# Second batch's shares of the last MLP pieces behind the other batch's, the very last product in two banks, and the plain output rows two to a step

## The chip, the cores and the metric

The kernel runs on one core of a Trainium2 chip. The metric is the device time of one execution in microseconds (us). The engines are TensorE (PE, with its weight loads as PEld), VectorE (DVE), ScalarE (ACT), GpSimd (POOL) and SyncE (SP), which here only issues DMAs.

## The reference, cut to what matters

Two layers on x of shape (2, 1024, 512): block-banded attention with a layer norm, then a routed layer. The routed layer picks 128 of 1024 rows of each batch, runs attention and a gated MLP on these 256 rows, mixes the result into the rows, and a second layer norm goes over everything. The change is in the MLP and behind it:

```
x1 = x + attn_out                                   # the 2 x 128 selected rows
h2 = _rms_norm(x1, ln2_w)
mlp = jax.nn.silu(h2 @ w_gate) * (h2 @ w_up) @ w_down   # 512 -> 2048 -> 512
processed = x1 + mlp
gated = gate * processed + (1.0 - gate) * x
output = hidden_states.at[b, idx].set(gated)        # the other rows stay as they are
return _layernorm(x + output)                       # over all rows
```

## The kernel before

The kernel writes the program of each engine itself. A planner calls `job(kind, key)` in one global order; each engine then walks through the jobs that have a part for it, in that order. So the order of the calls is the order of the work on every engine. `SIGNALS` lists the steps that a job completes on each engine, waits refer to them by name, and `hold`/`freed` make a job wait until the last user of a buffer or PSUM bank is done with it.

All products are made in three passes (high part by high part, high by low, low by high), so each float32 operand is split in two. A weight piece of 128 x 1024 is loaded by SP into one of three raw buffers (line 1893; the load of piece n waits for the low part of piece n - 3), rounded by ACT (line 1288), and the remainder is taken by POOL (line 1808) or DVE (line 1492), which alternate in the MLP.

The MLP (from `gate_up(c)` at line 753 and `down(c)` at line 764) has 8 steps c of 256 hidden columns. A step has a gate piece, an up piece, a down piece and two activation tiles, `gu` 2c and 2c + 1. For a tile TensorE makes gate and up for both batches (24 matmuls of 256 columns in bank proj0 or proj1). ACT applies silu (line 1470), DVE multiplies (line 1753), ACT rounds (line 1288), POOL takes the remainder (line 1855), all for 256 rows at once. `down(c)` then adds the two tiles of step c times piece `d2` c to the sums of batch 0 (bank s0) and batch 1 (bank s1), six matmuls of 512 columns for each. The planner calls `down(c - 1)` behind the tiles of step c, and `down(7)` last. In the stream of weight pieces, numbered through the whole kernel, step c has g2, u2 and then d2 of c - 1; the last ones are 84 (g2 of 7), 85 (u2 of 7), 86 (d2 of 6) and 87 (d2 of 7). POOL takes the low part of pieces with even numbers here, DVE that of odd ones. The high parts of the pieces that a step has loaded are planned at its end, behind the output row below.

Beside this, rows that were not selected go out: `plnorm` of batch 1 scales a tile of 128 rows on ACT (line 1384) and stores it (SP, line 1917, 256 KB). There are eight of them, `plain[0]` to `plain[7]`. Step c appends `plain[c]` to the running generators; two ticks later it is emitted, so tiles 0 to 4 go out at steps 2 to 6, and the last three behind `down(7)`.

The end: `fin` b on DVE adds the MLP sum of batch b to the residual already mixed (lines 1763, 1765, 1766: sum, statistics, aggregate), POOL makes the inverse root (lines 1781, 1783), `finrow` b on DVE normalises the row (line 1771), and POOL scatters the 128 rows of batch b (line 1868), after all stores of plain rows have landed. The jobs stand in the order fin 0, fin 1, finrow 0, finrow 1.

## Time and profile before

| | us |
|---|---|
| median of 3 runs | 1295.19 |
| lowest and highest | 1294.98, 1295.84 |
| the profiled execution's own time | 1295.61 |
| its span, from first to last instruction | 1293.8 |

In that execution TensorE was busy 98% of the span, VectorE 61%, ScalarE 46%, GpSimd 19%; its mean granted clock was 0.995 of full speed. Of the chain that ended last, 89% is TensorE and 5% DVE. The timeline rows read: start in us from the span's start, duration in us, engine, line of the kernel, operation, what it writes and reads with its shape, how many in a row, and in brackets how long the engine had been idle before and what released it. A row in which the same line occurs several times is merged.

### The profile page before, as it was taken

Reading aid. Unit: us, or ns where it says so; the run is one execution under the profiler, and the core shown is the slowest. Engines: PE = TensorE matmul, PEld = TensorE weight load, DVE = VectorE, ACT = ScalarE, POOL = GpSimd, SP = SyncE. Lnnn points to the kernel's source line nnn. Section 1 sums busy time; section 2 is a strip of 40 time slices with the busy share of each in tenths; the row PEclk is TensorE's granted clock in tenths of the full one; section 3 lists DMA queues with packets and bytes.
Section 4 is the critical chain, followed back from the end, with each engine's and each line's share of the span. In section 5 each row is a group of like instructions: output and inputs, shape, how many; then the busy total and the mean of one; then the engine's idle time right before and its main releaser. Section 6 shows DMA issues by size and latency. Waiting matters only on the chain.

```text
span 1293.8 us, 19096 instructions
## 1 busy us (share of the span) xinstructions
PE 1267.4 (98%) x7356; PEld 1091.0 (84%) x7356; DVE 784.0 (61%) x2189; ACT 600.5 (46%) x1424; POOL 244.2 (19%) x218
## 2 busy tenths in 40 slices
PE   9999999999999999999999999999999999999897
PEld 8898989898989898987789898989898985546696
DVE  5556565656665656667676766565655579744243
ACT  5544445454444444545544444444444443525353
POOL 2101111111111110224220202020201106100154
PEclk9999999999999999999999999999999999999899
DMA  6101101010101012013320100200010135582253
GB/s 203 34 17 33 34 33 33 30 37 20 47 17 50 33 50 65 17 41 115 109 95 17 49 18 13 75 33 34 27 32 26 35 123 177 190 287 96 88 190 138
DMA packets 62443, 89.34 MB, mean 69 GB/s; under 512 B 3264, under 2 KB 36032, under 8 KB 62352
## 3 DMA queue, kind: packets, MB, share of 16 engines
q1 hardware_dynamic: 61936, 86.82, 20.2%
q0 software_dynamic: 416, 1.31, 0.3%
q8 instruction: 57, 0.93, 0.3%
q14 instruction: 34, 0.28, 0.1%
HBM read 79.20 MB, written 8.91 MB: 68 GB/s over the span
## 4 chain that ended last, share of the span: by engine, by line
PE 89%; DVE 5%; ACT 3%; DMA 1%; issue 1%; POOL 0%; SPq 0%; POOLq 0%; ACTq 0%
PE proj L1008 42%; PE y L1008 13%; PE s L1008 10%; PE o L1008 9%; PE tp L1097 6%; PE proj L1016 4%; PE s L1016 2%; DVE arena L1492 2%; ACT arena L1288 1%; PE o L1016 1%; ACT prob L1326 1%; DVE products L1608 1%; DVE prob L1527 1%; DVE yacc L1579 1%; DMA late<-rope,position 1%
## 5 line engine op out<-in xcount | busy, mean ns | idle before, releaser
L1008 PE MATMUL proj<-arena 128*128 128x256 f32 (+1 forms) x3408 | 623.8, 332 | 2.9 <-DVE arena L1492 2.8
L1008 PEld LDWEIGHTS proj<-arena 128*128 128x128 f32 x3408 | 521.0, 190 | 60.0 <-DVE arena L1492 4.5
L1326 ACT ACTIVATE prob<-prob,stat 128x384 f32<-128x384 f32 (+1 forms) x256 | 151.0, 590 | 428.9 <-DVE stat L1527 428.9
L1808 POOL TENSOR_TENSOR arena<-wraw,arena 128x1024 fp32r<-128x1024 f32 x75 | 181.9, 2434 | 826.2 <-ACT arena L1288 826.2
L1492 DVE TENSOR_TENSOR arena<-proj,arena 128x512 fp32r<-128x512 f32 (+1 forms) x256 | 142.5, 557 | 267.6 <-ACT arena L1288 264.9
L1008 PE MATMUL y<-arena 128*128 128x512 f32 x810 | 210.7, 395 | 0.3 <-DVE yacc L1579 0.3
L1492 DVE TENSOR_TENSOR arena<-tp,arena 128x384 fp32r<-128x384 f32 (+2 forms) x258 | 134.7, 522 | 100.8 <-ACT arena L1288 100.5
L1008 PE MATMUL o<-arena 128*128 128x256 f32 (+2 forms) x960 | 194.6, 322 | 0.0
L1008 PE MATMUL s<-arena 128*128 128x384 f32 (+2 forms) x870 | 191.1, 333 | 2.2 <-DVE arena L1492 2.1
L1288 ACT ACTIVATE arena<-proj 128x512 fp32r<-128x512 f32 (+1 forms) x256 | 124.1, 485 | 114.9 <-PE proj L1008 111.9
L1008 PEld LDWEIGHTS y<-arena 128*128 128x128 f32 x810 | 146.6, 188 | 24.8 <-DVE yacc L1579 0.7
L1008 PEld LDWEIGHTS s<-arena 128*128 128x128 f32 x870 | 151.3, 188 | 19.1 <-DVE arena L1492 3.5
L1008 PEld LDWEIGHTS o<-arena 128*128 128x128 f32 x960 | 136.8, 190 | 0.7 <-DVE arena L1492 0.2
L1527 DVE CUSTOM_DVE_ANT_0 prob<-s,band 128x384 f32<-128x384 f32 (+1 forms) x256 | 131.6, 514 | 0.7 <-PE s L1008 0.7
L1288 ACT ACTIVATE arena<-tp 128x384 fp32r<-128x384 f32 (+2 forms) x258 | 118.0, 457 | 12.9 <-PE tp L1097 10.4
L1097 PE MATMUL tp<-ident,prob 128*128 128x128 f32 x704 | 119.3, 273 | 2.3 <-DVE prob L1536 2.3
L1536 DVE TENSOR_SCALAR prob<-prob,stat 128x384 f32<-128x384 f32 (+1 forms) x256 | 111.8, 437 | 9.1
L1097 PEld LDWEIGHTS tp<-ident,prob 128*128 128x128 f32 x704 | 85.9, 140 | 18.6 <-DVE prob L1536 7.8
L1579 DVE TENSOR_TENSOR yacc<-y,yacc 128x512 f32<-128x512 f32 x127 | 87.1, 686 | 13.6 <-PE y L1008 13.4
L1288 ACT ACTIVATE arena<-wraw 128x1024 fp32r<-128x1024 f32 (+1 forms) x90 | 91.0, 1036 | 5.8 <-DMA wraw<-in_L_ffn_w_gate 3.6
L1288 ACT ACTIVATE arena<-o 128x512 fp32r<-128x512 f32 (+1 forms) x74 | 42.1, 569 | 32.7 <-PE o L1179 22.7
L1016 PE MATMUL proj<-late 128*128 128x512 f32 x120 | 56.4, 598 | 0.0
(158 smaller groups left out, 691.1 us busy)
## 6 DMA issues: line engine op xcount, KB each, us to landing
wraw<-in_L_attn_Wv SPq DMA_DIRECT2D x16, 512.0 KB, 3.3
wraw<-in_L_attn_Wo SPq DMA_DIRECT2D x16, 512.0 KB, 3.7
late<-in_L_ffn_wq SPq DMA_DIRECT2D x16, 512.0 KB, 6.4
late<-in_L_ffn_wo SPq DMA_DIRECT2D x16, 512.0 KB, 4.7
wraw<-in_L_attn_Wq SPq DMA_DIRECT2D x15, 512.0 KB, 3.3
wraw<-in_L_attn_Wk SPq DMA_DIRECT2D x15, 512.0 KB, 3.4
yacc<-in_L_attn_hidden_states SPq DMA_DIRECT2D x16, 256.0 KB, 3.1
y_dram<-yacc SPq DMA_DIRECT2D x16, 256.0 KB, 3.1
```

Source lines behind the costliest of these rows:

```text
L1008: ins = e.matmul(out_ap, l[a], r[b], start=first and i == 0 and j == 0, stop=final and i == n - 1 and j == 2, skip_group_check=skip)
L1016: ins = e.matmul(out_ap, l, r, start=first and i == 0, stop=final and i == n - 1, skip_group_check=skip)
L1097: ins = e.transpose(bank["tp"][:, m * P:(m + 1) * P], prob[i % 2][:, m * P:(m + 1) * P], ident[:])
L1288: e.activation(dst, src, ACT.Copy).then_inc(*S_.inc(*name, "hi"))
L1326: e.activation(prob[s][:, 0:n], prob[s][:, 0:n], ACT.Exp, bias=stat[:, 4 * s + 1:4 * s + 2], scale=-1.0, accum_out=stat[:, 4 * s + 2:4 * s ...
L1492: e.tensor_tensor(dst_lo, src, dst_hi.bitcast(F32), ALU.subtract).then_inc(*V_.inc(*name, "lo"))
L1527: e.tensor_tensor_reduce(prob[s][:, 0:n], bank[f"s{s}"][:, 0:n], reach, -SCALE, -NEG, ALU.add, ALU.min, nm).then_inc(*V_.inc("scores", H, ...
L1536: e.tensor_scalar(prob[s][:, 0:n], prob[s][:, 0:n], rc, None, ALU.mult).then_inc(*V_.inc("norm", H, i, "prob"))
L1579: e.tensor_tensor(yacc[:, t, :], bank[bank_of["out", G, t]][:, :], yacc[:, t, :], ALU.add).then_inc(*V_.inc("out", G, t, "sum"))
L1608: e.tensor_tensor_reduce(products[:], row, router[:], 1.0, 0.0, ALU.mult, ALU.add, score[:, c:c + 1]).then_inc(*V_.inc("lnscore", b, t, "s ...
L1808: e.tensor_tensor(lo, wraw[n % RAW_SLOTS][:], hi.bitcast(F32), ALU.subtract).then_inc(*G_.inc("wsplit", n, "lo"))
```

## The change

The share of each batch in a down piece is a job of its own now: `down(b, c)`. For steps 1 to 5 the two shares follow each other as before. In step 6 only batch 0's share of piece 5 is planned, and in step 7 none. Behind the last tile come batch 1's share of piece 5, batch 0's shares of pieces 6 and 7, batch 1's of piece 6, and a new job `downend`: batch 1's product with piece 7, in two halves of 256 columns in two other banks (`y` and `o1`). On DVE, batch 1's sum is taken in three parts: `finsum` adds what bank s1 holds, `finend` adds each half and takes its statistics, and aggregates both. The plain rows are appended two to a step, in steps 0 to 3, so they are emitted two each at steps 2 to 5.

```diff
-        def down(c):
-            need("d2", 0, c)
+        def down(b, c):
+            if b == 0:
+                need("d2", 0, c)
             if c == 0:
-                for b in range(NB):
-                    hold(f"s{b}", ("down", 0), V_, "fin", b, "sum")
-            job("down", c)
-            retire(("d2", 0, c), "down", c, f"made{NB - 1}")
+                hold(f"s{b}", ("down", b, 0), V_, "finsum" if b else "fin", b, "sum")
+            job("down", b, c)
+            if b == NB - 1:
+                retire(("d2", 0, c), "down", b, c, "made")
...
         for c in range(FF // GW):
             gate_up(c)
-            if c >= 1:
-                down(c - 1)
+
+            if 1 <= c < FF // GW - 1:
+                down(0, c - 1)
+            if 1 <= c < FF // GW - 2:
+                down(1, c - 1)
             was_loaded = loaded_to[0]
             tick()
-            running.append([plain[c], None])
+            for t in range(2 * c, min(2 * c + 2, TT)):
+                running.append([plain[t], None])
             split_loaded(was_loaded)
-        down(FF // GW - 1)
+        down(1, FF // GW - 3)
+        for c in (FF // GW - 2, FF // GW - 1):
+            down(0, c)
+        down(1, FF // GW - 2)
+
+
+        for half, to in enumerate(ENDS):
+            hold(to, ("downend", half), V_, "finend", 1, ("left", "right")[half])
+        job("downend")
...
+                elif kind == "downend":
+                    c = FF // GW - 1
+                    w2 = [z.rearrange("p (k n) -> p k n", k=2) for z in weights("d2", 0, c)]
+                    pe.wait_ge(*split("d2", 0, c))
+                    pe.wait_ge(*G_.at("gu", 2 * c + 1, "lo"))
+                    for half, name in ((0, "left"), (1, "right")):
+                        cols = slice(half * GW, (half + 1) * GW)
+                        pe.wait_ge(*freed(ENDS[half], "downend", half))
+                        ins = three_passes(e, bank[ENDS[half]][:, cols],
+                                           [([aT[(2 * c + f) % A_SLOTS][z][:, P:2 * P] for z in range(2)],
+                                             [w2[z][:, f, cols] for z in range(2)]) for f in range(2)], True, True)
+                        ins.then_inc(*T_.inc("downend", name))
...
+                elif kind == "finend":
+                    b, = key
+                    y1 = work[4 + b]
+                    dve.wait_ge(*V_.at("finsum", b, "sum"))
+                    dve.wait_ge(*freed(f"moments{b}", "finend", b))
+                    dve.wait_ge(*freed(f"share{b}", "finend", b))
+                    for half, name in ((0, "left"), (1, "right")):
+                        cols = slice(half * GW, (half + 1) * GW)
+                        dve.wait_ge(*T_.at("downend", name))
+                        after(e.scalar_tensor_tensor(y1[:, cols], bank[ENDS[half]][:, cols], gate[:, 4 * b + 1:4 * b + 2], y1[:, cols],
+                                                     ALU.mult, ALU.add), "finend", b, name)
+                        after(e.bn_stats(halves[:, 6 * half:6 * half + 6], y1[:, cols]), "finend", b, f"{name}stats")
+                    e.bn_aggr(mv[b][:], halves).then_inc(*V_.inc("finend", b, "moments"))
```

TensorE from the tiles of step 6 (12 and 13) to its last instruction, before. proj0 and proj1 are the tiles, s0 and s1 the sums of batch 0 and 1:

```order
L1008 MATMUL proj0<-arena 128x256 x24
L1008 MATMUL proj1<-arena 128x256 x24
L1008 MATMUL s0<-arena 128x512 x6
L1008 MATMUL s1<-arena 128x512 x6
L1008 MATMUL proj0<-arena 128x256 x24
L1008 MATMUL proj1<-arena 128x256 x24
L1008 MATMUL s0<-arena 128x512 x6
L1008 MATMUL s1<-arena 128x512 x6
L1008 MATMUL s0<-arena 128x512 x6
L1008 MATMUL s1<-arena 128x512 x6
```

The same of the changed kernel (its line 1031 is line 1008 of before):

```order
L1031 MATMUL proj0<-arena 128x256 x24
L1031 MATMUL proj1<-arena 128x256 x24
L1031 MATMUL s0<-arena 128x512 x6
L1031 MATMUL proj0<-arena 128x256 x24
L1031 MATMUL proj1<-arena 128x256 x24
L1031 MATMUL s1<-arena 128x512 x6
L1031 MATMUL s0<-arena 128x512 x12
L1031 MATMUL s1<-arena 128x512 x6
L1031 MATMUL y<-arena 128x256 x6
L1031 MATMUL o1<-arena 128x256 x6
```

One share of s1 stands behind the last two tiles, the shares of s0 stand ahead of the last one of s1, and the last product of batch 1 goes to y and o1.

ACT from the tiles of step 5 to its last instruction, before. `works<-yacc` is an output row, `arena<-wraw` a high part of a weight piece:

```order
L1384 ACTIVATE works<-yacc,stat 128x512
L1288 ACTIVATE arena<-wraw2 128x1024
L1288 ACTIVATE arena<-wraw0 128x1024
L1288 ACTIVATE arena<-wraw1 128x1024
L1470 ACTIVATE works<-proj0 128x256
L1288 ACTIVATE arena<-works 128x256
L1470 ACTIVATE works<-proj1 128x256
L1288 ACTIVATE arena<-works 128x256
L1384 ACTIVATE works<-yacc,stat 128x512
L1288 ACTIVATE arena<-wraw2 128x1024
L1288 ACTIVATE arena<-wraw0 128x1024
```

The same place of the changed kernel (its lines are 35 higher):

```order
L1419 ACTIVATE works<-yacc,stat 128x512 x2
L1323 ACTIVATE arena<-wraw2 128x1024
L1323 ACTIVATE arena<-wraw0 128x1024
L1323 ACTIVATE arena<-wraw1 128x1024
L1505 ACTIVATE works<-proj0 128x256
L1323 ACTIVATE arena<-works 128x256
L1505 ACTIVATE works<-proj1 128x256
L1323 ACTIVATE arena<-works 128x256
L1323 ACTIVATE arena<-wraw2 128x1024
L1323 ACTIVATE arena<-wraw0 128x1024
```

Two output rows stand ahead of the three high parts, at this step and at the three before it; ahead of the last two high parts (pieces 86 and 87) stands none, and none behind the last tile, where three stood.

DVE behind the last tile, before and then of the changed kernel:

```order
L1763 SCALAR_TENSOR_TENSOR works<-s0,gate,works 128x512
L1765 BN_STATS bn_out0<-works 128x6
L1766 BN_AGGR mv0<-bn_out0 128x2
L1763 SCALAR_TENSOR_TENSOR works<-s1,gate,works 128x512
L1765 BN_STATS bn_out1<-works 128x6
L1766 BN_AGGR mv1<-bn_out1 128x2
```

```order
L1820 SCALAR_TENSOR_TENSOR works<-s0,gate,works 128x512
L1822 BN_STATS bn_out0<-works 128x6
L1823 BN_AGGR mv0<-bn_out0 128x2
L1796 SCALAR_TENSOR_TENSOR works<-s1,gate,works 128x512
L1808 SCALAR_TENSOR_TENSOR works<-y,gate,works 128x256
L1810 BN_STATS stat<-works 128x6
L1808 SCALAR_TENSOR_TENSOR works<-o1,gate,works 128x256
L1810 BN_STATS stat<-works 128x6
L1811 BN_AGGR mv1<-stat 128x2
```

The sum of s1 stands alone now, and two half sums with half statistics follow it ahead of batch 1's aggregate.

## Rows read from the trace of the kernel before

**Rows 1.** The page's first line: the span of the profiled execution.

```profile
span 1293.8 us, 19096 instructions
```

**Rows 2.** Chain of waits that ended last: start, duration (us), engine, output, line, count.

```profile
1209.01 0.70 DVE works L1729
...
1214.32 14.42 PE proj L1008 x96
...
1271.24 2.75 PE s L1008 x12
1273.99 5.75 PE proj L1008 x48
1279.74 4.12 PE s L1008 x18
...
1283.89 0.76 DVE works L1763
...
1284.67 0.70 DVE bn_out L1765
...
1285.58 0.65 DVE works L1763
...
1286.98 0.19 DVE mv L1766
...
1288.51 1.31 POOL out L1868
```

**Rows 3.** Timeline of ACT, steps 2 to 6 of the MLP.

```profile
1239.15 1.99 ACT L1288 ACTIVATE arena<-wraw 128x1024 fp32r<-128x1024 f32 x2
...
1249.59 1.06 ACT L1288 ACTIVATE arena<-wraw 128x1024 fp32r<-128x1024 f32 x1 [0.90 <-DMA wraw<-in_L_ffn_w_gate]
...
1256.08 0.71 ACT L1384 ACTIVATE works<-yacc,stat 128x512 f32<-128x512 f32 x1
1256.69 1.99 ACT L1288 ACTIVATE arena<-wraw 128x1024 fp32r<-128x1024 f32 x2
...
1267.47 1.06 ACT L1288 ACTIVATE arena<-wraw 128x1024 fp32r<-128x1024 f32 x1 [1.77 <-DMA wraw<-in_L_ffn_w_gate]
```

**Rows 4.** Timeline of DVE: low parts of 75, 79, 85, 87; product of tile 15.

```profile
1241.18 2.59 DVE L1492 TENSOR_TENSOR arena<-wraw,arena 128x1024 fp32r<-128x1024 f32 x1 [3.00 <-ACT arena L1288]
...
1252.08 2.13 DVE L1492 TENSOR_TENSOR arena<-wraw,arena 128x1024 fp32r<-128x1024 f32 x1 [2.13 <-ACT arena L1288]
...
1269.92 2.17 DVE L1492 TENSOR_TENSOR arena<-wraw,arena 128x1024 fp32r<-128x1024 f32 x1 [2.97 <-ACT arena L1288]
...
1276.60 2.58 DVE L1492 TENSOR_TENSOR arena<-wraw,arena 128x1024 fp32r<-128x1024 f32 x1 [3.00 <-ACT arena L1288]
...
1280.26 0.42 DVE L1753 TENSOR_TENSOR works<-works,proj 128x256 f32<-128x256 f32 x1 [0.75 <-ACT works L1470]
```

**Rows 5.** Timeline of POOL: low parts of 84, of 86, and of tile 15.

```profile
1268.60 2.41 POOL L1808 TENSOR_TENSOR arena<-wraw,arena 128x1024 fp32r<-128x1024 f32 x1 [3.64 <-ACT arena L1288]
...
1275.69 2.40 POOL L1808 TENSOR_TENSOR arena<-wraw,arena 128x1024 fp32r<-128x1024 f32 x1 [0.82 <-ACT arena L1288]
...
1281.21 0.74 POOL L1855 TENSOR_TENSOR arena<-works,arena 128x256 fp32r<-128x256 f32 x1 [0.43 <-ACT arena L1288]
```

**Rows 6.** Timeline of SP: the issue of the load of piece 84.

```profile
1261.32 0.37 SPq L1893 DMA_DIRECT2D wraw<-in_L_ffn_w_gate  x1
```

**Rows 7.** Timeline of PE: two matmul groups that came after idle time.

```profile
1140.14 0.66 PE L1179 MATMUL o<-ident,works 128*128 128x128 f32 x4 [1.44 <-DVE works L1676]
...
1212.28 0.63 PE L1179 MATMUL o<-ident,works 128*128 128x128 f32 x4 [3.31 <-DVE works L1739]
```

**Rows 8.** Stretches: window and length, busy us per engine, granted clock, DMA share, GB/s.

```profile
1140.00:1141.00 1.00, 0.86 (x5) 0.69 (x6) 0.08 (x1) 0.17 (x1) 0.00 (x0) 1.00 1.05 387
...
1214.32:1216.00 1.68, 1.68 (x8) 1.68 (x9) 1.09 (x2) 0.52 (x1) 0.00 (x0) 0.50 0.00 0
...
1266.00:1267.00 1.00, 1.00 (x10) 1.00 (x9) 0.96 (x1) 0.00 (x0) 0.00 (x0) 1.00 0.91 324
```

More of the change, by code:

```diff
@@ L290, in build @@
         twice = stat[:, 8:8 + TT]
+        halves = stat[:, 20:32]
         router = sb("router", [P, D])
@@ L950, in build @@
         for b in range(NB):
-            hold(f"moments{b}", ("fin", b), V_, "finrow", b, "row")
-            hold(f"share{b}", ("fin", b), V_, "finrow", b, "row")
-            job("fin", b)
+            last = ("finend" if b else "fin", b)
+            hold(f"moments{b}", last, V_, "finrow", b, "row")
+            hold(f"share{b}", last, V_, "finrow", b, "row")
+            if b == 1:
+                job("finsum", b)
+            job(*last)
         for b in range(NB):
```

42 lines of the change are left out of this document (26 added, 16 removed).

## The prediction, made before the changed kernel was run

> **What bounds the kernel now.** I read the page first: the span is 1293.8 us [rows 1]. The profiled execution took 1295.61 us, so 1.81 us lie around the span; the three timed runs have a median of 1295.19 us, 0.42 us under it. Everything the change touches lies in the last 80 us, so the next view is the chain of waits that ended last [rows 2]. It shows two regimes. Up to 1283.87 the chain is TensorE without a gap: 5.75 us for two gate/up tiles (48 matmuls of 256 columns, 0.120 each), 2.75 us for one down piece (12 of 512 columns, 0.229 each, so 1.375 us for one batch's share). Then comes a tail off TensorE: DVE sums, takes statistics and aggregates for batch 0, then for batch 1, until 1287.17; POOL makes the root, DVE the last row, and POOL scatters. The last share of batch 1 is TensorE's last work. The chain row holds 18 of the last 24 matmuls, so six more (1.375 us) end at 1285.24, while DVE is busy with batch 0. The end of the aggregate of batch 1, 1287.17 now, sets everything behind it, since POOL scatters batch 0 only after batch 1's root. So the question is where that 1287.17 goes.
>
> Then I read the engines' timelines [rows 3 to 6] for what TensorE will want earlier than before. A weight piece goes load (SP), high part (ACT), low part (POOL or DVE), product. I number the pieces as the stream does: 84 and 85 are the last gate and up pieces, 86 and 87 the last two down pieces. TensorE starts the last pair of gate/up tiles at 1273.99 in the chain; the low part of piece 85 was done at 1269.92 + 2.17 = 1272.09 [rows 2, 4]: slack 1.9 us. The low part of activation tile 15 was done at 1281.21 + 0.74 = 1281.95 [rows 5]; the last down piece wants it at 1279.74 + 2.75 = 1282.49: slack 0.54 us.
>
> **Part 1: batch 1's share of piece 5 moves behind tile 15.** TensorE's work is the same, but the last pair of tiles can start 1.375 us sooner, at 1271.24 + 1.375 = 1272.62. The two slacks shrink by as much: 1.9 becomes 0.53, and the second can become a wait, because tile 15's activation does not follow TensorE. Its chain is: DVE finishes the split of piece 87 (1276.60 + 2.58 = 1279.18) and only then multiplies tile 14, ACT rounds, DVE multiplies tile 15 at 1280.26, and POOL ends at 1281.95 [rows 4, 5]. The split of 87 in turn ends 1.09 us after POOL's split of 86 (1275.69 + 2.40 = 1278.09); the same lag stands at 85 behind 84 (1272.09 against 1268.60 + 2.41 = 1271.01, 1.08 us) [rows 4, 5]. So tile 15's low part follows piece 85's low part by 1281.95 - 1272.09 = 9.86 us, 0.61 of which is an output row of ACT (below) that the change takes out of this stretch: 9.25 us.
>
> Three shares now stand between tile 15 and its first use: batch 1 of piece 5, batch 0 of piece 6, then batch 0 of piece 7, which waits. Without any other shift the wait would be over at 1272.09 + 9.25 = 1281.34, and TensorE would come at 1272.62 + 5.75 + 2 x 1.375 = 1281.12: a stall of 0.22 us.
>
> **Part 2: the output rows.** Eight rows of batch 1 (ACT, then a store of 256 KB on SP) stood one to a step, the last three at the end; now two each stand at the steps of tiles 4 to 11, and none later. ACT does them ahead of the high parts. One more row costs 0.61 us (1256.08 to the next operation at 1256.69 [rows 3]). It is hidden only where ACT would wait otherwise. Step by step: at 1239.15 the high parts of pieces 74 and 75 go 0.61 us later, so DVE's low part of 75 (ends 1243.77 [rows 4]) and the load of 78 that waits for it do too. The next high part is one for which ACT waits on that load (0.90 us at 1249.59 [rows 3]), so the delay stays: 0.61. POOL's and DVE's splits hang on it, up to 1254.21 [rows 4], and DVE multiplies tile 8 only behind them; 1.87 us later ACT reaches its rows. There the second extra row is added: 1.22 us. The high parts at 1256.69, their splits, and the load of 84 at 1261.32 [rows 6] are 1.22 us late. Piece 84 arrives 6.15 us after its issue (1267.47, ACT waits 1.77 us for it [rows 3]). The extra rows of the next step are covered by that wait. TensorE has 0.7 us or more to spare in all steps before. So piece 85's low part comes at 1272.09 + 1.22 = 1273.31. The stores add 0.26 MB to each burst; here I take it that they delay no load issued before them.
>
> On that last point the trace is not decisive: 84 was issued behind another load and took 6.15 us, which fits either sharing or queueing. The Trainium skill, page "DMA: Bandwidth & Descriptors", section "Queues, rings and completion order", says that on each DMA engine descriptors are consumed in ring order; by it an added store delays nothing issued ahead of it on the same queue. By the opposite reading the loads would come up to 0.7 us later, which is the third case below.
>
> **Sum for TensorE.** The last pair of tiles starts at 1273.34 instead of 1272.62 (a stall of 0.7). The share that waits for tile 15 starts at 1273.31 + 9.25 + 0.03 = 1282.6, where TensorE would be at 1273.34 + 8.5 = 1281.84 (a second stall of 0.75). Behind it: its own 1.375, batch 1 of piece 6 with 1.375, and the last product in halves, 12 matmuls of 256 columns at 0.120 = 1.44 (six of 512 cost 1.375, so 0.06 more). TensorE ends at 1286.8, 1.5 us later than now.
>
> **Part 3: the tail on DVE.** Batch 0's share ends at 1282.6 + 1.4 = 1284.0. From there DVE does: batch 0's sum, statistics and aggregate, 1285.58 - 1283.89 = 1.69; batch 1's first sum, 0.65; twice a half sum and half statistics; an aggregate, 0.19. No row shows these halves. A two-input operation takes 0.70 with 512 columns [rows 2] and 0.42 with 256 [rows 4]; the half sum is then 0.76 - 0.28 = 0.48 at most, 0.42 at least, and I take 0.45; half statistics, 0.70 with 512 columns [rows 2] like that operation, 0.42. Together 2 x 0.87 + 0.03 x 3 = 1.83, less 0.06 where one overlaps the next. The aggregate then ends at 1284.0 + 1.69 + 0.65 + 1.77 + 0.19 = 1288.3. TensorE's end alone would allow 1286.8 + 0.02 + 0.45 + 0.42 + 0.19 + gaps = 1287.95, so DVE is what is late next, by 0.35. If the halves cost nothing beyond half their work, 0.6 us less; if they cost as much as a full one, about 1.1 us more. That bounds this term.
>
> The Trainium skill, page "VectorE: DVE Perf Modes", section "The TRN2 errata", speaks against this part: many small tiles pay a fixed cost each, and it advises tiles of at least 512 elements. The rows above already show that cost (0.14 us fixed in 0.42 and 0.70), so it is in the sum; taken as a verdict, the split would cost more than it gives, by those 0.3 us of extra DVE time.
>
> The aggregate moves from 1287.17 to 1288.3: 1.15 us later. Everything behind it (root, last row, two scatters [rows 2]) is the same work in the same order and moves along. The last plain store no longer ends near the scatter, but the scatter did not wait for it, so that gives nothing. Span 1294.95 us, the profiled execution 1296.75, and against the median **1296.3 us**.
>
> **The rivals.**
> - *The rows are absorbed.* If ACT's delays are eaten up by the waits for loads (landings that come no later although issued later), piece 85 keeps 1272.09. TensorE stalls 0.2 us, batch 0's share starts at 1281.37, and the aggregate ends 1.22 us earlier than in my sum, 1287.1: 0.1 us faster than now, 1295.1. With halves at their cheapest 0.6 us faster, 1294.6. For it: ACT waits 0.90 and 1.77 us for loads [rows 3]. Against it: those loads are issued by splits that are themselves late.
> - *The stores share with the loads.* Pieces 78 and 84 land later by some of the 0.8 us that 0.26 MB takes at about 320 GB/s [rows 8]; the shift is 1.6 to 1.9 instead of 1.22, and the time 1296.7 to 1297.0.
> - *The clock falls (the slower side).* The stalls are new idle time on TensorE. Before 1212.28 the engine had been idle for 3.31 us, and in the stretch behind the granted clock was 0.50, that is 1.2 GHz [rows 7, 8]; the 96 matmuls from there took 14.42 us [rows 2] where two pairs of tiles take 11.5. If one of the new stalls did the same the time would be 1296.3 + 2.9 = 1299.2, slower by 0.3%. It decides where a stall comes near those 3.3 us; after one of 1.44 us at 1140.14 the clock stayed at 1.00, 2.4 GHz [rows 7, 8], and I expect stalls under 1 us.
> - *The split does what it is meant to.* No shift by the rows and cheap halves, TensorE's end decides: at best 0.9 us faster, 1294.3.
>
> **Numbers.** Chances: my forecast 0.5; rows absorbed 0.22; stores share 0.15; clock or another stall above 1.5 us 0.07; the split as meant 0.06. A measurement of this kernel can tell about 0.2% (2.6 us) from no change, and all cases but the clock lie inside. The cases with no row shift reach down to 1294.3, those with shared bandwidth and a dearer tail to 1297.6; the runs before spread by 0.9 us. Range 1294.4 to 1297.5. Faster by over 0.2% would need 2.6 us, more than the whole wait between TensorE's end and the aggregate (1.93 us) that can be shortened: 0.03. Slower by over 0.2%: 0.08. Within: 0.89.
>
> **What would show it.** Right: in the timeline of after a gap of about 0.7 us on TensorE before the last pair of gate/up tiles, with DVE's low part of piece 85 as releaser; a second of about 0.75 us before batch 0's last share, released by POOL; the gate piece's high part at about 1268.7 instead of 1267.47; the two half sums directly behind each other on DVE with TensorE already done; clock 1.00 throughout. Wrong: no gap before the last pair (rows absorbed); POOL's root for batch 1 earlier than now; half operations of other lengths than 0.42 to 0.48; a granted clock of 0.50 behind one of the stalls.

## The result, and the profile after

| | before | changed |
|---|---|---|
| median of 22 runs each, us | 1295.52 | 1297.49 |
| lowest and highest | 1293.27, 1297.52 | 1294.77, 1299.9 |
| ratio of the times | | 1.0016, 95% interval 1.001 to 1.0022 |

That is 2.07 us slower, 1.3 to 2.85. The forecast was 1.1 us slower (1296.3): the direction held, the size did not quite. The changed kernel was timed twice more beside the kernel before, on chips 2 and 15: ratios 1.0005 (0.9996 to 1.0014) and 1.0008 (0.9999 to 1.0017). Weighted by the width of their intervals the three give 1.0012, with about 0.0004 to either side: 1.5 us, 0.9 to 2.1.

The span of the profiled execution is no help here:

```profile
span 1293.7 us, 19113 instructions
```

It is within 0.1 us of that of before [rows 1], though the times differ. Single executions of one kernel differ by 4 to 5 us, and the granted clock goes with it: of the 22 executions of the changed kernel the four with a mean granted clock of 0.997 took 1294.77 to 1295.51 us, the five with 0.994 took 1297.31 to 1299.90. The fifteen traces of this study show two places.

The first lies about 135 us ahead of the MLP. In every trace TensorE waits there for 2.06 to 2.09 us, until 1077.6 to 1078.7. In eight of them (changed_again, changed_third, rows_only, rows_old, rows_odd, one_bank, spread_one_bank, small_stores) the granted clock falls to 0.50 behind it for a few us, in seven (before and changed among them) it stays at 1.00. The same stretch in before, then in changed_again (columns as in [rows 8]):

```profile
1080.00:1083.00 3.00, 3.00 (x13) 1.88 (x12) 2.76 (x9) 2.14 (x3) 2.11 (x6) 1.00 0.49 177
```

```profile
1080.00:1083.00 3.00, 3.00 (x8) 1.92 (x7) 2.40 (x9) 1.29 (x3) 2.11 (x6) 0.51 0.53 170
```

In those eight the MLP's first matmul starts at 1214.78 to 1215.97, in the other seven at 1213.63 to 1214.32. The second place is the MLP's first row of tiles. It starts 0.35 us earlier here than before and takes 13.28 us, where it took 14.42 [rows 2], since the clock stayed at 0.50 for longer in the trace of before. The stretch from 1218 to 1219, before and then changed:

```profile
1218.00:1219.00 1.00, 1.00 (x7) 1.00 (x7) 0.00 (x0) 0.00 (x0) 0.00 (x0) 0.50 0.00 0
```

```profile
1218.00:1219.00 1.00, 1.00 (x11) 1.00 (x10) 0.00 (x0) 0.35 (x1) 0.00 (x0) 1.00 0.00 0
```

In all traces the stretch from that start to the third pair of tiles took 15.66 to 17.01 us, the kernel before having the longest. The change does not touch either place, and behind batch 1's aggregate all fifteen traces take 6.61 to 6.64 us to the end of the span. So I read a **stage** in every run: from the start of tile 4 (the third pair of gate/up tiles) to the end of batch 1's aggregate. Before, it starts at 1231.33 and ends at 1287.16: 55.83 us. After, it starts at 1229.83.

Timeline of PE after (start us, duration us, then as in [rows 7]), from the last but one pair of gate/up tiles:

```profile
1263.83 5.92 PE L1031 MATMUL proj<-arena 128*128 128x256 f32 x48
1269.59 1.55 PE L1031 MATMUL s<-arena 128*128 128x512 f32 x6
1271.91 6.02 PE L1031 MATMUL proj<-arena 128*128 128x256 f32 x48 [0.78 <-DVE works L1788]
1277.77 2.91 PE L1031 MATMUL s<-arena 128*128 128x512 f32 x12
1280.92 3.00 PE L1031 MATMUL s<-arena 128*128 128x512 f32 x12 [0.24 <-POOL arena L1912]
1283.76 0.88 PE L1031 MATMUL y<-arena 128*128 128x256 f32 x6
1284.47 0.88 PE L1031 MATMUL o<-arena 128*128 128x256 f32 x6
```

Two stalls, at the two places forecast. Back to back the last pair would start at 1269.59 + 1.375 = 1270.96; it starts 0.95 us later. The printed 0.78 is shorter because a row's duration runs on to the last matmul's visible end: six matmuls of 512 columns take 1.375 in a stream and show 1.55. The second: 1271.91 + 5.75 + 2.75 = 1280.41 would be back to back, and it is 1280.92, another 0.51. Of this 0.11 is not waited: the pair of tiles behind the first wait takes 5.86 us to the next row (1271.91 to 1277.77) instead of 5.75.

Timeline of DVE behind the last tile, after; the end of the last row is the end of the stage:

```profile
1282.58 0.75 DVE L1820 SCALAR_TENSOR_TENSOR works<-s,gate,works 128x512 f32<-128x512 f32 x1 [3.07 <-PE s L1031]
...
1284.20 0.72 DVE L1796 SCALAR_TENSOR_TENSOR works<-s,gate,works 128x512 f32<-128x512 f32 x1
1284.95 0.48 DVE L1808 SCALAR_TENSOR_TENSOR works<-y,gate,works 128x256 f32<-128x256 f32 x1
1285.47 0.43 DVE L1810 BATCH_NORM_STATS2 stat<-works 128x6 f32<-128x256 f32 x1
1285.93 0.48 DVE L1808 SCALAR_TENSOR_TENSOR works<-o,gate,works 128x256 f32<-128x256 f32 x1
1286.45 0.43 DVE L1810 BATCH_NORM_STATS2 stat<-works 128x6 f32<-128x256 f32 x1
1286.91 0.21 DVE L1811 BATCH_NORM_AGGREGATE mv<-stat 128x2 f32<-128x12 f32 x1
```

The stage ends at 1287.12 and lasts 57.29 us, 1.46 more than before. From the start of batch 0's sum DVE needs 4.54 us here; before, 1283.89 to 1287.16, 3.27 [rows 2]. It is never idle between, and TensorE has finished both halves when DVE comes to the second.

The stretches show that no clock is behind it (columns as in [rows 8]): the granted clock is 1.00 right behind both stalls, 2.4 GHz; the 0.50 of the MLP's start is the same as in [rows 8].

```profile
1271.90:1273.00 1.10, 1.09 (x9) 1.09 (x10) 0.39 (x1) 0.68 (x2) 0.61 (x1) 1.00 0.78 270
1281.00:1282.00 1.00, 1.00 (x5) 0.82 (x6) 0.00 (x0) 0.00 (x0) 0.00 (x0) 1.00 0.00 0
```

### The profile page after: what moved, and what is told of

It reads as the page before. It is cut to its first block, busy times and chain, and to the rows that moved or that the text cites. A ratio compares the mean times of both kernels' runs of the same rounds, so it can differ in the third digit from the quotient of the medians.

```text
span 1293.7 us, 19113 instructions
## 1 busy us (share of the span) xinstructions
PE 1267.3 (98%) x7362; PEld 1090.4 (84%) x7362; DVE 785.1 (61%) x2192; ACT 600.6 (46%) x1424; POOL 244.6 (19%) x218
## 4 chain that ended last, share of the span: by engine, by line
PE 85%; DVE 6%; ACT 4%; DMA 2%; POOL 2%; issue 1%; SPq 0%; ACTq 0%; POOLq 0%
PE proj L1031 39%; PE y L1031 13%; PE o L1031 9%; PE s L1031 9%; PE tp L1120 6%; PE proj L1039 4%; DVE arena L1527 3%; PE s L1039 2%; ACT arena L1323 2%; DMA wraw<-in_L_ffn_w_up 1%; POOL arena L1865 1%; PE o L1039 1%; DVE products L1643 1%; ACT prob L1361 1%; DVE prob L1562 1%
```

## The experiments

All runs in one table, in us. Everything but the time is counted in the stage, from the start of tile 4. "low 85" is the end of the low part of piece 85, "low tile 15" that of the last activation tile, "sum 0" the start of DVE's sum of batch 0, "tail" from there to the end of batch 1's aggregate. "waits" are the gaps that the PE timeline prints. The ratio is to the kernel before on the same chip, with its 95% interval. small_stores, split_end_alone and split_later have a trace and no comparison of times.

| run | low 85 | low tile 15 | waits | sum 0 | tail | stage | ratio |
|---|---|---|---|---|---|---|---|
| before | 40.76 | 50.62 | none | 52.56 | 3.27 | 55.83 | |
| changed | 41.70 | 50.94 | 0.78, 0.24 | 52.75 | 4.54 | 57.29 | 1.0016 (1.001 to 1.0022) |
| changed_again | 41.67 | 50.92 | 0.75, 0.25 | 52.73 | 4.53 | 57.26 | 1.0005 (0.9996 to 1.0014) |
| changed_third | 41.26 | 50.51 | 0.35, 0.24 | 52.32 | 4.54 | 56.86 | 1.0008 (0.9999 to 1.0017) |
| rows_only | 41.26 | 50.62 | none | 52.57 | 3.27 | 55.84 | 0.9998 (0.9989 to 1.0006) |
| rows_old | 40.47 | 50.34 | 0.67 | 52.14 | 4.54 | 56.68 | 0.9998 (0.9989 to 1.0007) |
| rows_odd | 41.59 | 50.84 | 0.46, 0.26 | 52.64 | 4.54 | 57.18 | 1.0008 (0.9999 to 1.0016) |
| one_bank | 41.50 | 50.75 | 0.59, 0.26 | 52.55 | 4.48 | 57.03 | 1.0009 (1.0001 to 1.0018) |
| spread_rows | 39.67 | 49.26 | none | 51.20 | 4.53 | 55.73 | 0.999 (0.9981 to 0.9999) |
| spread_again | 39.58 | 49.26 | none | 51.20 | 4.54 | 55.74 | 1.0001 (0.9992 to 1.001) |
| spread_one_bank | 39.72 | 49.26 | none | 51.20 | 4.49 | 55.69 | 0.9999 (0.999 to 1.0008) |
| small_stores | 42.18 | 51.43 | 1.27, 0.24 | 53.24 | 4.53 | 57.77 | |
| split_end_alone | 40.26 | 50.63 | none | 52.56 | 4.54 | 57.10 | |
| split_later | 39.22 | 49.37 | none | 51.23 | 4.54 | 55.77 | |
| spread_whole_end | 40.46 | 49.71 | none | 51.50 | 4.41 | 55.91 | 0.9994 (0.9985 to 1.0003) |

My theory was that of the prediction: the rows push piece 85 late, the new order has no slack for it, and the longer DVE tail costs its own. The rivals: the tail is late only because TensorE is; the waits come from stores sharing with loads; or the order itself costs something.

**rows_only.** The kernel before with the rows two to a step.

```diff
-            running.append([plain[c], None])
+            for t in range(2 * c, min(2 * c + 2, TT)):
+                running.append([plain[t], None])
```

> The kernel before with the plain rows two to a step at steps 2 to 5, and nothing else. Measure: the stage from the first matmul of tile 4 (start of the third pair of gate/up tiles on TensorE) to the end of batch 1's aggregate on DVE, which is 55.84 us before and 57.30 us in the changed kernel. Theory A (the extra rows make the weight pieces late, and only the earlier need for them turns that into stalls): the low part of the last up piece comes 0.9 us later counted from tile 4 (41.7 instead of 40.8 us), TensorE waits for nothing, since 1.9 us of slack stand there, and the low part of tile 15 comes 0.3 us later with 0.5 of slack: stage 55.8, time equal to before within 0.3 us. Rival B (the stores or rows cost time wherever they stand): stage 56.5 or more, time 0.7 to 2 us above before.

Low 85 came 0.5 us later, not the 0.9 expected, and nothing else moved: stage 55.84 against 55.83. In the old order the rows cost nothing, since TensorE comes 1.375 us later to the last pair.

**rows_old.** The changed kernel with the rows one to a step, as before.

```diff
-            for t in range(2 * c, min(2 * c + 2, TT)):
-                running.append([plain[t], None])
+            running.append([plain[c], None])
```

> The changed kernel with the plain rows one to a step, as before the change. Stage as in rows_only: 55.84 before, 57.30 changed. Theory A (half of the loss is the rows, the other half the wait for tile 15's low part, which does not come sooner though TensorE does): the last up piece is back at 40.8 us from tile 4 and the pair of tiles behind batch 0's share of piece 5 starts without a gap; the wait ahead of batch 0's last share grows to 0.8 to 1.0 us, because one output row stands again in ACT's way to the last down pieces; stage 56.9 to 57.0, 1.1 above before. Rival B (the rows are the whole loss): no wait above 0.2 us, stage 55.7 to 56.1, time equal to before.

The first wait is gone, the second is longer: one row stands in its old place, on ACT between the last pieces, so low tile 15 follows low 85 by 9.87 us again (9.86 before, 9.24 in the changed kernel).

```profile
1277.57 2.91 PE L1030 MATMUL s<-arena 128*128 128x512 f32 x12
1281.15 3.00 PE L1030 MATMUL s<-arena 128*128 128x512 f32 x12 [0.67 <-POOL arena L1911]
```

That is the PE timeline of this run. Stage 56.68: the rows' part in the 1.46 us is 0.6, and 0.85 are left without it. The time does not resolve either, and one trace of each is thin: against changed_third (56.86) the rows' part is only 0.2. That rows in these places do push low 85 shows over all traces: with the rows as before it is 39.22 to 40.76 (before, rows_old, split_end_alone, split_later), with two to a step 41.26 to 42.18 (changed three times, rows_only, one_bank, small_stores).

**rows_odd.** The changed kernel with two rows at once in each of steps 0, 1, 3 and 5, where ACT was expected to have room.

```diff
-            tick()
-            for t in range(2 * c, min(2 * c + 2, TT)):
-                running.append([plain[t], None])
+            if c in (0, 1, 3, 5):
+                put(plain.pop(0), plain.pop(0))
```

> The changed kernel with the plain rows in pairs at steps 0, 1, 3 and 5, where ACT waits for loads anyway, and none at steps 2 and 4. Theory A (weight pieces set both stalls): the last up piece's low part comes 0.3 to 0.9 us earlier than before the change (39.9 to 40.5 us from tile 4), no gap ahead of the last pair of tiles, at most 0.2 us ahead of batch 0's last share; batch 0's sum starts at 51.2 to 51.4 us, DVE needs 4.55 us from there: stage 55.8 to 56.0, 1.3 to 1.5 less than the changed kernel and equal to before. Rival B (the stalls come from the stores' traffic, which is the same in sum): both stalls stay within 0.3 us, stage 57 or more.

This missed: both waits stayed, stage 57.18. SP's timeline of this run shows what the placement overlooked:

```profile
1226.79 0.97 SPq L1973 DMA_DIRECT2D out<-works  x2
1227.80 1.49 SPq L1949 DMA_DIRECT2D wraw<-in_L_ffn_w_down  x1
1229.34 0.47 SPq L1949 DMA_DIRECT2D wraw<-in_L_ffn_w_gate  x1
```

The stores of step 0 stand ahead of three loads in SP's order and are issued first; in the kernel before the gate load of this place was issued at 1226.54. The loads of the following pieces come 1 to 3.5 us later than before, and as each load waits for a split that waits for a load, it carries on: low 85 is late by about as much as in the changed kernel. This is read from the order of the issues; no run tests it by itself. spread_rows below, with no row in step 0, has neither the waits nor loads that late, but its other rows stand differently too.

**one_bank.** The changed kernel with batch 1's last product whole, in one bank, and one sum and one statistics behind it. `finsum` stays.

```diff
-                    for half, name in ((0, "left"), (1, "right")):
-                        cols = slice(half * GW, (half + 1) * GW)
...
+                    pe.wait_ge(*freed(ENDS[0], "downend", 0))
+                    ins = three_passes(e, bank[ENDS[0]][:, :],
...
+                    ins.then_inc(*T_.inc("downend", "left"))
```

> The changed kernel with the very last product undivided: six matmuls of 512 columns into one bank, one sum, one statistics, one aggregate. In the changed kernel DVE takes 4.55 us from batch 0's sum to batch 1's aggregate and is never idle. Theory A (DVE, not TensorE, is late at the end, so halves buy nothing): TensorE ends 2.75 us after batch 0's share, DVE waits for it 0.4 us and then takes 1.7: 4.48 us, stage 57.2, 0.1 less than the changed kernel. Rival B (the halves save what they are meant to): stage 57.8 or more, 0.5 us longer. Rival C (the halves cost their fixed part twice on the path): stage 56.9 or less.

The tail is 4.48 instead of 4.54 us. In the DVE timeline of this run DVE waits for TensorE, and saves as much in work:

```profile
1287.31 0.75 DVE L1803 SCALAR_TENSOR_TENSOR works<-y,gate,works 128x512 f32<-128x512 f32 x1 [0.45 <-PE y L1030]
1288.10 0.69 DVE L1805 BATCH_NORM_STATS2 stat<-works 128x6 f32<-128x512 f32 x1
```

Two halves cost 1.96 us with their gaps (1284.95 to 1286.91 above), one whole 1.51 (1287.31 to 1288.82). The second bank takes away 0.45 us of waiting and adds 0.45 us of work and a longer aggregate. It also shows what the rest of the longer tail is: without its 0.45 us of waiting this tail has 4.03 us of work, 0.76 more than before. That is the one sum more that batch 1 needs when its last product goes to another bank than the rest, whole or in halves.

**spread_rows.** The changed kernel with the rows where they delay no piece on its way to the last pair: two in steps 1, 3 and 5, one in step 2, one behind the last product.

```diff
-            tick()
-            for t in range(2 * c, min(2 * c + 2, TT)):
-                running.append([plain[t], None])
+            for _ in range({1: 2, 2: 1, 3: 2, 5: 2}.get(c, 0)):
+                put(plain.pop(0))
...
-        while running:
-            tick()
+        put(plain.pop(0))
```

> The changed kernel with the plain rows where ACT waits for loads and no store stands ahead of an urgent load: two at steps 1, 3 and 5, one at step 2, one behind the last tile, none at steps 4 and 6. Theory A (the weight pieces' lateness is what the row at step 4 and the doubled row at step 2 put on them): the last up piece is ready 40.1 to 40.8 us after tile 4 starts, no gap ahead of the last pair of tiles, tile 15's low part 9.24 us behind it, a wait of at most 0.2 us ahead of batch 0's last share; stage 55.7 to 56.1, 1.2 to 1.6 less than the changed kernel and no better than before by more than 0.15. Rival B (even with all stalls gone the loss stays, as in rows_odd): stage 57 or more.

PE, timeline of this run:

```profile
1269.04 1.55 PE L1029 MATMUL s<-arena 128*128 128x512 f32 x6
1270.43 5.92 PE L1029 MATMUL proj<-arena 128*128 128x256 f32 x48
1276.18 5.63 PE L1029 MATMUL s<-arena 128*128 128x512 f32 x24
```

Both waits are gone, and batch 0's sum starts 1.36 us sooner than before, which is the share that moved behind (1.375). The stage is only 0.10 us shorter than before: the tail, 4.53 against 3.27, takes 1.26 of it. This is the change working as it is meant to, and it is worth a tenth of a microsecond.

**spread_one_bank.** spread_rows and one_bank together.

> spread_rows with the very last product undivided in one bank. Theory A (DVE's 4.48 us with one bank against 4.55 with two): stage 0.0 to 0.1 less than spread_rows, 55.6 to 56.0, so that neither form of the last product beats before by more than 0.2 us. Rival B (with the stalls gone TensorE's end matters and two banks win 0.4 or more): stage 56.2 or more.

Stage 55.69 against 55.73: also without stalls the second bank brings nothing.

**small_stores.** The changed kernel, but the stores of batch 1's plain rows write 8 of 512 columns, so their bytes are left out (4 KB a store instead of 256).

```diff
-                    e.dma_start(out[b, t * P:(t + 1) * P, :], work[2 + t % 2][:]).then_inc(out_stored[t % 2].sem, 16)
+                    w = 8 if b == NB - 1 else D
+                    e.dma_start(out[b, t * P:(t + 1) * P, 0:w], work[2 + t % 2][:, 0:w]).then_inc(out_stored[t % 2].sem, 16)
```

> The changed kernel in which each store of a plain row of batch 1 writes 8 of 512 columns (4 KB in place of 256 KB), so those rows of the output are left out; ACT's rows stay. Theory A (loads are late because they are issued late; stores issued behind them do not hold them up): the last gate and up loads land 5.8 and 5.4 us after their issue, as in the changed kernel, within 0.3, and the low part of the last up piece at 41.5 to 41.8 us from tile 4. Rival B (stores share the DMA engines with loads issued ahead of them): the last up load lands 0.7 us or more sooner after its issue, and the gap ahead of the last pair of tiles shrinks from 0.78 to 0.3 us or less.

The last gate and up loads landed 6.0 and 5.2 us after their issue, in the changed kernel 5.8 and 5.4; both waits are there, the first of 1.27 us. So the stores' bytes did not hold up the loads ahead of them; the number of stores is the same, so this says nothing of what an issue costs. Two rows of the issues from 1255 to 1275 (what is written and read, engine, operation, count, size, median us to landing), first small_stores, then changed:

```profile
wraw<-in_L_ffn_w_gate SPq DMA_DIRECT2D x1, 512.0 KB, 6.0
out<-works SPq DMA_DIRECT2D x4, 4.0 KB, 2.8
```

```profile
out<-works SPq DMA_DIRECT2D x4, 256.0 KB, 4.1
wraw<-in_L_ffn_w_gate SPq DMA_DIRECT2D x1, 512.0 KB, 5.8
```

Why low 85 is 0.5 us later than in the changed kernel, this one trace does not show.

**split_end_alone.** The kernel before, with its order and its rows; only the very last product goes to two banks, with `finsum` and `finend`.

```diff
-            if 1 <= c < FF // GW - 1:
+            if 1 <= c:
                 down(0, c - 1)
-            if 1 <= c < FF // GW - 2:
                 down(1, c - 1)
...
-            for t in range(2 * c, min(2 * c + 2, TT)):
-                running.append([plain[t], None])
+            running.append([plain[c], None])
             split_loaded(was_loaded)
-        down(1, FF // GW - 3)
-        for c in (FF // GW - 2, FF // GW - 1):
-            down(0, c)
-        down(1, FF // GW - 2)
+        down(0, FF // GW - 1)
```

The edit is shown against the changed kernel.

> The kernel before, with its order of the shares and of the output rows; only batch 1's very last product goes to two banks in halves, and DVE takes batch 1's sum in three parts. Counted from the start of the third pair of gate/up tiles to the end of batch 1's aggregate (the stage, 55.83 us before, 57.29 in the changed kernel). Theory (the longer DVE tail is a cost of its own, whatever stands ahead): no wait on TensorE, batch 0's sum starts at 52.5 to 52.6 as before, DVE needs 4.5 us from there instead of 3.27, stage 57.1. Rival (the tail is long only because TensorE's last shares come late in the changed order): DVE 3.9 or less, stage 56.5 or less.

Batch 0's sum starts at 52.56 as before, the tail is 4.54, the stage 57.10: the longer tail costs 1.27 us by itself, with no wait of TensorE. DVE, timeline of this run, first and last operation of the tail:

```profile
1282.22 0.75 DVE L1815 SCALAR_TENSOR_TENSOR works<-s,gate,works 128x512 f32<-128x512 f32 x1 [3.21 <-PE s L1026]
...
1286.55 0.21 DVE L1806 BATCH_NORM_AGGREGATE mv<-stat 128x2 f32<-128x12 f32 x1
```

**split_later.** rows_old, with the split of piece 87 planned behind tile 14.

```diff
+                if ft == 14:
+                    split_loaded(len(stream))
...
-            split_loaded(was_loaded)
+            split_loaded(min(was_loaded, len(stream) - 1))
```

> The changed order of the shares and the two banks, with the output rows one to a step as before, and the split of the last weight piece (87) planned behind tile 14's product, so that on ACT, DVE and POOL it no longer stands ahead of the two last activation tiles. With the rows alone put back, TensorE waited 0.67 us for the low part of tile 15 (50.34 us into the stage), and batch 0's sum started at 52.14. Theory (the second wait comes from the split of piece 87 standing ahead of the activations): the low part of tile 15 comes at 49.9 to 50.0, the wait is 0.3 us or less, batch 0's sum starts at 51.3 to 51.6 and the stage is 55.9 to 56.2. Rival (the activation chain itself is the limit): low part of tile 15 at 50.3, the wait stays at 0.6 to 0.7, stage 56.7.

The wait is gone altogether and batch 0's sum starts at 51.23, more than either had said. Low tile 15 is at 49.37, since not only the order changed. The DVE timeline of this run:

```profile
1274.19 0.42 DVE L1789 TENSOR_TENSOR works<-works,proj 128x256 f32<-128x256 f32 x1 [3.84 <-ACT works L1506]
1276.05 1.23 DVE L1528 TENSOR_TENSOR arena<-wraw,arena 128x1024 fp32r<-128x1024 f32 x1 [1.43 <-ACT arena L1324]
```

The same split took 2.46 us in the changed kernel, where POOL's split ran beside it, and 2.58 before [rows 4]. Here POOL was done with its own at 1274.85, and DVE needs half the time. But the run does not settle what removed the wait. Low 85 is at 39.22 here: the load of piece 84 was issued 0.53 us sooner in the stage than before, and ACT had it 5.12 us after its issue instead of 6.15. With the 9.87 of rows_old behind it low tile 15 would have come at 49.09, in time as well. And there is a floor: even where no split holds it up, tile 15's low part ends 2.37 us behind the last tile on TensorE (46.89 to 49.26 in spread_rows, 48.25 to 50.62 before).

**spread_again, changed_third.** spread_rows and the changed kernel once more, on one further chip.

> The same kernel as spread_rows (the changed order and banks; output rows spread so that none delays a weight piece), on another chip and in more rounds. Theory (the stage decides: 55.73 against 55.83 us before): the time is within 0.5 us of the kernel before, ratio 0.9996 to 1.0004, and the 0.999 of the first comparison was chance. Rival: it is 1 us or more faster, ratio under 0.9992, and something outside the stage gains.

> The changed kernel once more against the kernel before. Theory (the stage decides: 57.29 against 55.83 us, +1.45): ratio 1.0009 to 1.0013, between the 1.0016 and the 1.0005 of the two comparisons so far. Rival (something outside the stage costs 0.6 us more): 1.0016 or above.

spread_again has the same stage to 0.01 us and a ratio of 1.0001: the 0.999 of the first comparison was not repeated. changed_third came to 1.0008, a little below what its theory gave, with a first wait of 0.35 and a stage of 56.86; the stage of this kernel is thus 56.9 to 57.3, by how the weight loads land. changed_again, for which I had written:

> The changed kernel once more, unaltered, for a second trace and a second comparison with before. Theory A (the loss is what the stage from tile 4 to batch 1's aggregate shows, 57.30 against 55.84 us): the stage comes out at 57.2 to 57.5 again with the same two gaps, and the time 1.0 to 1.9 us above before. Rival B (something outside the stage adds 0.5 us or more in most executions): stage as before, time 2 us or more above before.

gave 1.0005 and a stage of 57.26.

**spread_whole_end.** spread_rows, but batch 1's last product whole, into s1 like all others, and its end on DVE as before the change.

```diff
         down(1, FF // GW - 2)
...
-        for half, to in enumerate(ENDS):
-            hold(to, ("downend", half), V_, "finend", 1, ("left", "right")[half])
-        job("downend")
...
+        down(1, FF // GW - 1)
...
-            if b == 1:
-                job("finsum", b)
```

> The changed order of the shares with the output rows spread as in spread_rows, but batch 1's very last product whole, into s1 as before, and its sum, statistics and aggregate in one piece each on DVE. Theory (in spread_rows the end was DVE's: 4.53 us of work from the start of batch 0's sum at 51.20; in the kernel before it had 3.27): batch 0's sum starts at 51.2, DVE is done with batch 0 at 52.9 and then waits for TensorE, whose last share ends at 54.0 as before; 1.65 us of sum, statistics and aggregate follow, so the stage is 55.6 us, set by TensorE. The earlier batch 0 is worth nothing more than 0.2 us, and the time is within 0.5 us of the kernel before. Rival (the shares in the new order cost TensorE itself something): its last share ends after 54.3 and the stage is 55.9 or more.

DVE, timeline of this run:

```profile
1281.53 0.75 DVE L1812 SCALAR_TENSOR_TENSOR works<-s,gate,works 128x512 f32<-128x512 f32 x1 [3.06 <-PE s L1023]
1282.31 0.69 DVE L1814 BATCH_NORM_STATS2 bn_out<-works 128x6 f32<-128x512 f32 x1
1283.04 0.18 DVE L1815 BATCH_NORM_AGGREGATE mv<-bn_out 128x2 f32<-128x6 f32 x1
1284.25 0.75 DVE L1812 SCALAR_TENSOR_TENSOR works<-s,gate,works 128x512 f32<-128x512 f32 x1 [1.02 <-PE s L1023]
```

Batch 0 is done early and DVE then stands idle for 1.02 us: with the old tail TensorE's end is the bound. The stage came to 55.91, on the number of the rival, but not for its reason: TensorE's last matmul ended at 54.18 in the stage, under the rival's 54.3 (53.88 before). Low tile 15 was at 49.71 here; TensorE would want it at 46.89 + 2.75 = 49.64, and starts some 0.15 behind the low part, so about 0.2 to 0.3 us were waited (too short for a bracket, in a row of 30 matmuls). That is the 0.3 by which batch 0's sum, 51.50, misses 51.2. Without it the stage would be the 55.6 that the theory gives.

Nothing here beats the kernel before by an amount that can be measured. The shortest stage is 55.69 against 55.83.

## Why the prediction was right or wrong, point by point

**The books of the stage.** The step of the prediction that failed is the tail of Part 3, which was 0.24 us too short; the stalls came out right in sum, though the first had another releaser than the one forecast. Each term stands alone in a run:

| term | forecast | measured | from |
|---|---|---|---|
| batch 0's shares one share ahead | -1.375 | -1.36 | spread_rows against before |
| stalls and what follows them | +1.5 | +1.55 | changed against spread_rows, start of batch 0's sum |
| DVE from batch 0's sum to batch 1's aggregate | +1.0 | +1.27 | split_end_alone against before |
| sum | +1.15 | +1.46 | changed against before |

**The tail was mis-sized, by 0.24 us.** That is most of the 0.31 us error in the stage. The sum was 1.69 + 0.65 + 1.77 + 0.19 = 4.30 and the trace has 4.54: 1.70 for batch 0, 0.67 for the first sum, 1.96 for the halves, 0.21 for the aggregate. The halves were the term that no row showed. I took 0.45 for a half sum and 0.42 for half statistics, and had 0.03 three times as distance between them; they are 0.48 and 0.43 with about 0.04 behind each, 0.98 for a half. The half sum was at the upper end of the bound that I had worked out for it (0.48). Why it takes 0.06 more than the product with 0.42 is open: that product reads a PSUM bank too (proj), and differs in the kind of operation. I had also taken off 0.06 for an overlap that the trace does not have between halves that depend on each other. The size of the whole term comes from the sum in one more part: one_bank has 0.76 of the 1.27 us, the cut in halves brings the rest and saves TensorE's wait.

**The first stall was forecast with another releaser, and came out near by luck.** The last pair of tiles was to start at 1273.34, 42.01 us into the stage, and starts at 42.08: two errors cancel. The shift of piece 85 was to be 1.22 us and is 0.94 in this trace. Its first part held: in SP's timeline after, the load of piece 84 is issued 31.27 us into the stage, before 1261.32 - 1231.33 = 29.99 [rows 6], 1.28 late. But it landed 5.80 us after issue instead of 6.15.

```profile
1261.10 0.39 SPq L1950 DMA_DIRECT2D wraw<-in_L_ffn_w_gate  x1
```

ACT's high part of it came 0.93 later than before [rows 3]. The up piece's high part came 1.46 later (1268.83 in the kernel before), and low 85 still only 0.94, since it ends 1.09 us behind POOL's split of 84 (1270.44), as it did before (1.08). In ACT's timeline after:

```profile
1266.90 1.06 ACT L1323 ACTIVATE arena<-wraw 128x1024 fp32r<-128x1024 f32 x1 [1.68 <-DMA wraw<-in_L_ffn_w_gate]
1268.79 1.06 ACT L1323 ACTIVATE arena<-wraw 128x1024 fp32r<-128x1024 f32 x1 [0.83 <-DMA wraw<-in_L_ffn_w_up]
```

How much of the shift was absorbed is not settled: changed_again has 0.91, changed_third 0.50, and low 85 of one placement of rows scatters by 0.4 us and more.

Against that, I had TensorE start 0.03 us behind the low part of piece 85, and it starts 0.38 behind. What it waits for is the next operation on DVE. Tile 14 needs bank proj0 free, and DVE's product of tile 12, which frees it, is queued behind that low part. The chain of waits after shows it:

```profile
1269.88 1.65 DVE arena L1527
1271.53 0.34 DVE works L1788
```

So the slack of the last pair of tiles before was not the 1.9 us that I read off the low part: the product of tile 12 ended at 1272.43, 1.4 us ahead of the start of the tiles in the PE timeline (1273.83). The new order alone, 1.375, takes nearly all of it. I had looked at the operand that comes late, and not at the bank that stands behind it in the same queue. The stall itself is 0.95 and not 0.7, for a third error: I counted from 1273.99, where the chain puts the pair, while its first matmul started at 1273.83, so the point without a stall was 0.16 too late (0.72 - 0.28 + 0.35 + 0.16 = 0.95).

**The second stall** came where it was forecast, released by POOL, with the distance from piece 85 to tile 15 at 9.24 (forecast 9.25). The waiting matmuls started 0.14 behind the low part, not 0.03. It was 0.51, not 0.75, since piece 85 was less late and the first stall had already taken more. Its size follows low 85 and what stands between: in rows_old one row of 0.61 there lengthens the distance to 9.87. But the prediction's "tile 15's activation does not follow TensorE" holds only where low 85 is late. Over the traces (split_later, with its own order, aside) low tile 15 is the later of two: 9.24 (9.87 with the row) behind low 85, or 2.37 behind TensorE's last tile. Before, both came to 50.62; in split_end_alone and rows_only low 85 moved by 1 us, 40.26 and 41.26, and low tile 15 stayed at 50.63 and 50.62. In the spread runs with 49.26 it is TensorE's too. That the split of piece 87 is what holds the distance at 9.24 is read from the queues and not separately shown (split_later).

**The rivals.** The rows absorbed (0.22): no; low 85 came 0.50 to 0.94 later. Stores sharing with the loads (0.15): no, small_stores. The Trainium skill's page "DMA: Bandwidth & Descriptors", section "Queues, rings and completion order", has descriptors consumed in ring order on each DMA engine, from which I had drawn that an added store delays nothing issued ahead of it. These runs agree, with 5.8 us to landing with 256 KB stores behind the load and 6.0 with 4 KB. The clock (0.07): no, 1.00 behind both stalls. But the case was told too simply: I had the clock fall only behind stalls near 3.3 us, and behind the 2.07 us ahead of 1078 it fell in eight traces of fifteen, so a stall of that length is not safe; the ones here were under 1 us. The split as meant (0.06): not even where no wait is in its way; spread_rows gains 0.10 where the best case had 0.9. The warning against many small tiles of the Trainium skill's page "VectorE: DVE Perf Modes", section "The TRN2 errata", fits: I had counted 0.3 us of DVE time for it, and one_bank shows 0.45 us, all that the second bank gives.

**The time.** The stage explains 1.46 us, and the three comparisons together measured 1.5 (0.9 to 2.1). The first alone gave 2.07 (1.3 to 2.85), which holds 1.46 as well. Of the 1 us between forecast and first measurement 0.3 us is the stage. The rest is open. Ahead of and behind the stage the traces show no cost of the change, and the clock's falls ahead of the MLP can move a comparison by as much, but the traces are too few to say how often each kernel has them. That the rest is chance of this comparison fits the two others and is not shown by anything else. The forecast's 1296.3 was also set against a median of 3 runs that was itself 0.33 us under the one of 22.

## What to carry to other kernels

Moving work out from ahead of a step takes its slack away: before that, list everything the step waits for, its free output bank too, and what is queued ahead of the releaser on its engine. A sum that is taken in one more part to start earlier costs a whole pass more: 0.76 us here. An operation cut in halves to hide a wait must gain more than its second start costs; here 0.45 us of waiting was bought with 0.45 us of work. Where single executions differ by more than the effect, measure a stage between two fixed events in the trace; it repeated to 0.01 us in spread_rows and 0.4 us in the changed kernel, where the ratios of the same two kernels moved by 1.4 us.

## What the runs showed of the hardware that I had not expected

- DVE's split of a 128 x 1024 piece takes 1.23 us when POOL is idle. When POOL's split (2.41 us) runs, it ends 1.08 to 1.09 us behind POOL's, as in 1270.44 and 1271.53 after, whenever it started itself: 1.65, 2.13, 2.46 and 2.59 us are all the same work. I had used the 1.08 as a number of this kernel without seeing what it was. The Trainium skill, page "SBUF — State Buffer", section "SBUF: two separate sides", has the two engines share a pair of ports under an exclusive lock: a DVE operation with two SBUF inputs and a GpSimd operation that reads SBUF exclude each other, and the later one is blocked until the other ends. The trace agrees. So by these rows a split given to the second engine at the same time ends both after 2.41 + 1.08 = 3.49 us, where one behind the other would take 2.41 + 1.23 = 3.64 by my estimate, and it holds up whatever is queued behind it on DVE.
- The first group of matmuls behind a wait starts 0.14 us after its releaser's end, and batch 0's sum starts 1.66 us after that group's start (1280.92 to 1282.58), where in a stream without a wait it is 1.57 (in spread_rows 46.88 + 2.75 = 49.63 to 51.20).
- The same wait of TensorE, 2.06 to 2.09 us long and ahead of the same work, was followed by a granted clock of 0.50 in eight traces and of 1.00 in seven. The MLP starts 0.46 to 2.34 us later in the eight.
- The stretch behind TensorE's 3.31 us of idle time ahead of the MLP [rows 7], in which the clock is granted at 0.50 at first, takes 15.66 to 17.01 us to the third pair of tiles with the same work on TensorE. With both places, tile 4 starts at 1229.29 to 1231.97 over all traces: 2.68 us of the 4 to 5 by which executions of one kernel differ.
